# Local attention: scores of eight heads at once in contractions of 64 rows, and GpSimd's sum of the queries held back

## The reference, cut to what matters

```python
h = shift_token(x)
q, k, v = split(h @ wqkv)                      # 8 heads of 64
q = l2norm(q) * qs; k = l2norm(k) * ksc
q, k = rotary_xpos(q, k)
sim = einsum('bhwid,bhwjd->bhwij', 8 * q, k)   # a window of 64 queries, its own and the previous 64 keys
attn = softmax(where(mask, -max, sim))
x = x + (attn @ v) @ wo
```

## Time and profile before

| | us |
|---|---|
| median of 3 runs | 2175.99 |
| lowest and highest | 2174.62, 2183.37 |
| the profiled execution | 2176.2 |
| its span (first to last instruction) | 2174.4 |
| TensorE, VectorE, ScalarE, GpSimd busy in the span | 1781.2, 1635.1, 1271.2, 957.9 |
| local transformer, about | 1297 to 2174 of the span |

### The profile page before, as it was taken

The page is one execution under the profiler, slowest core; times in us unless marked ns, Lnnn a source line. Parts: engine busy times, 40 slices in busy tenths (PEclk is TensorE's granted clock), DMA queues, the critical chain, the costliest instruction groups (busy, mean ns, idle before and its releaser), DMA issues. The chain is left out here.

```text
span 2174.4 us, 36880 instructions
## 1 busy us (share of the span) xinstructions
PE 1781.2 (82%) x12448; PEld 976.1 (45%) x12448; DVE 1635.1 (75%) x3467; ACT 1271.2 (58%) x2737; POOL 957.9 (44%) x773
## 2 busy tenths in 40 slices
PE   5888898865889998859943757999998899999875
PEld 2333333332344444424423424655655556566543
DVE  5999999995577777622235767999986689999775
ACT  5777877740344444414434236888884388888721
POOL 5777887761012222223431245555550255555311
PEclk8999999996899999959976878999999999999997
DMA  5333333312111111114235140000001000000010
GB/s 150 110 111 119 122 108 116 93 49 81 39 37 36 41 36 44 31 41 133 65 105 165 52 137 15 16 21 16 11 16 23 13 16 21 16 16 11 15 42 23
DMA packets 107401, 125.47 MB, mean 58 GB/s; under 512 B 28804, under 2 KB 79151, under 8 KB 106224
## 3 DMA queue, kind: packets, MB, share of 16 engines
q1 hardware_dynamic: 103120, 115.07, 18.7%
q0 software_dynamic: 4096, 8.06, 1.1%
HBM read 71.60 MB, written 38.11 MB: 50 GB/s over the span
## 5 line engine op out<-in xcount | busy, mean ns | idle before, releaser
L394 POOL TENSOR_TENSOR m_bu<-m_dtu,m_brow 128x1024 f32<-128x1024 f32 x128 | 299.8, 2358 | 55.6 <-DVE m_hs L818 53.9
L818 DVE TENSOR_TENSOR_SCAN m_hs<-m_ps_da,m_bu 128x1024 f32<-128x1024 f32 x128 | 292.3, 2283 | 3.0 <-POOL m_bu L394 2.5
L1363 ACT ACTIVATE a_pt<-a_ps_s 128x1024 f32<-128x1024 f32 x128 | 131.1, 1024 | 226.7 <-PE a_ps_s L1141 226.7
L523 PE MATMUL m_ps_y_ps<-m_prod,m_ident 128*128 128x512 f32 x512 | 243.1, 597 | 0.0
L2913 ACT ACTIVATE l_pe<-l_ps_s,l_nbias,l_qs 128x128 f32<-128x128 f32 x512 | 227.9, 459 | 1.6
L1480 DVE TENSOR_REDUCE a_mpad<-a_ps_s 128x4 f32<-128x1024 f32 x128 | 156.9, 1226 | 92.3 <-PE a_ps_s L1133 91.1
L1133 PE MATMUL a_ps_s<-a_heads 32*128 32x256 f32 x1024 | 187.5, 446 | 43.6 <-DVE a_mpad L1480 28.5
L670 ACT ACTIVATE m_ps_da<-m_dt,m_a_neg 128x510 f32<-128x510 f32 x256 | 166.0, 681 | 74.3 <-DVE m_hs L818 73.4
L1141 PE MATMUL a_ps_s<-a_qm,a_heads 32*128 32x256 f32 x1024 | 184.7, 437 | 1.8 <-ACT a_pt L1363 1.4
L1067 POOL TENSOR_TENSOR a_rstd<-a_ve,a_mhalf 128x2 f32<-128x2 f32 x48 | 33.8, 705 | 303.0 <-DVE a_ve L1438 163.3
L828 DVE TENSOR_TENSOR m_prod<-m_hs,m_ps_c_ps 128x1024 f32<-128x1024 f32 x128 | 153.6, 1200 | 12.1 <-PE m_ps_c_ps L509 12.1
(11 more groups left out here) (339 smaller groups left out, 4252.1 us busy)
## 6 DMA issues: line engine op xcount, KB each, us to landing
m_brow<-state_rows SPq DMA_DIRECT2D x64, 512.0 KB, 4.3
slots<-m_void SPq DMA_DIRECT2D x16, 516.0 KB, 5.4
l_near<-l_v SPq DMA_DIRECT2D x64, 128.0 KB, 2.3
e_xs<-slots SPq DMA_DIRECT2D x16, 258.0 KB, 2.8
ys<-m_void SPq DMA_DIRECT2D x8, 512.0 KB, 5.3
qk<-a_qk SPq DMA_DIRECT2D x16, 256.0 KB, 2.0
a_heads<-qk SPq DMA_DIRECT2D x64, 64.0 KB
ew_w<-in_w SPq DMA_DIRECT2D x2, 2048.0 KB, 11.8
```

The source lines that it names most:

```text
L394: nc.gpsimd.tensor_tensor(bu[s % 4][:, :, :], dtu[p][:, :, :], b2, ALU.mult).then_inc(bu_rd, 1)
L523: last = pe.matmul(y_ps[:, h, :], ident[:, :], prod[d % 3][:, h, :], start=False, stop=(s == NS - 1))
L818: dve.tensor_tensor_scan(hs[s % 4][:, :, :].rearrange("p h t -> p (h t)"), da[s % 2][:, :, :, :].rearrange("p h q t -> p (h q t)"), bu[s % ...
L1363: nc.scalar.activation(pt[t % 2][:, :, :], s2[:, :, :], ACT.Exp).then_inc(exp_rd, 1)
```

## The change

- `scores` makes all 8 heads of a chunk. `kT` loses its second plane and its zeros. Each head is its own contraction over its 64 rows: even heads (rows 0 to 63) go to the first bank of `s_ps`, odd heads (64 to 127) to the second, first and second alternating. The first chunk has 8 such products of 128 by 128, the second 16 of 64 result rows by 128 columns. Two masks are written first.
- `k_copy` is one copy of 128 partitions. The clears of `kT` are gone.
- `maxima` is one reduce of 8 heads from two banks and one product. `exps` still runs in units of four, but needs the maxima of all eight, and the next `scores` needs the exponentials of all eight.
- GpSimd's `rotary_sum` of block b waits also until VectorE has done the first division of the same chunk of block b - 1.
- The `attend` lists of TensorE, ScalarE and VectorE are in a new order, and so is the end of a layer: ScalarE copies the output of the first chunk of the last block before `p_copy` of its unit U - 2, and VectorE has both last divisions ahead of `norm_apply`.

The diff; unchanged lines, small count changes and ScalarE's and VectorE's old `attend` lists are left out:

```diff
@@ -2442,10 +2442,10 @@
-kT = [m.sb(f"kT{i}", [P, 2, NP, T]) for i in range(2)]
+kT = [m.sb(f"kT{i}", [P, NP, T]) for i in range(2)]
-top, nbias = m.sb("top", [P, HU]), m.sb("nbias", [P, 2, HU])
+top, nbias = m.sb("top", [P, NH]), m.sb("nbias", [P, NH])
@@ -2467,10 +2467,10 @@
-s_ps = [m.ps(f"s{i}") for i in range(2)]
+s_ps = m.ps("s", (P, 2, 512))
-h_ps = s_ps + t_ps
+h_ps = [s_ps[:, 0, :], s_ps[:, 1, :]] + t_ps
@@ -2542,13 +2542,13 @@
         last.then_inc(cleared, 1)
         for i in range(2):
             nc.gpsimd.memset(hT[i][:, 0:1], 0.0).then_inc(cleared, 1)
-        for i in range(2):
-            nc.gpsimd.memset(kT[i][:, :, :, :], 0.0).then_inc(cleared, 1)
         def rotary_sum(l, b, c):
             i = NCH * b + c
             pool.wait_ge(l.rot_rd[Q], i + 1)
+            if b > 0:
+                pool.wait_ge(l.pn_rd, U * (b - 1) + NU * c + 1)
             nc.gpsimd.tensor_tensor(c1[Q][:, :, :], c1[Q][:, :, :], c2[Q][:, :, :], ALU.add).then_inc(l.sum_rd[Q], 1)
         def query_norms(l, b, c):
@@ -2642,26 +2642,28 @@
                                     c1[K][:, 2 * j:2 * j + 2, :].rearrange("p h d -> p (h d)"), ident[:, :])
             last.then_inc(l.xT_mm[K], 1)
-        def scores(n, b, u):
-            l, p, c, d = at[n], b % 2, u // NU, u % NU
-            i = U * b + u
-            if d == 0:
-                pe.wait_ge(l.xT_sb[Q], NCH * b + c + 1)
-                pe.wait_ge(l.xT_sb[K], 2 * (NCH * b + c + 1))
-            at_least(pe, l.ex_rd, HU * (i - 1))
-            bank = s_ps[u % 2][:, :].rearrange("p (h k) -> p h k", h=HU)
-            pe.matmul(bank, identb[:, :], mask[:, c, :, :], start=True, stop=False, skip_group_check=True)
-            for k in range(2):
-                j = 2 * d + k
+        def scores(n, b, c):
+            l, p, i = at[n], b % 2, NCH * b + c
+            pe.wait_ge(l.xT_sb[Q], i + 1)
+            pe.wait_ge(l.xT_sb[K], i + 1)
+            at_least(pe, l.ex_rd, NH * i)
+            bank = [s_ps[:, r, :].rearrange("p (j t) -> p j t", j=NP) for r in range(2)]
+            side = [slice(r * HD, (r + 1) * HD) for r in range(2)]
+            for r in range(2):
+                pe.matmul(bank[r], identb[:, :], mask[:, c, :, :], start=True, stop=False, skip_group_check=True)
+            for j in range(NP):
                 if c == 0:
-                    last = pe.matmul(bank[:, 2 * k:2 * k + 2, :], qT[p][:, j, 0:P], kT[p][:, :, j, 0:P],
-                                     start=False, stop=True, skip_group_check=True)
+                    for r in range(2):
+                        last = pe.matmul(bank[r][:, j, :], qT[p][side[r], j, 0:P], kT[p][side[r], j, 0:P],
+                                         start=False, stop=True, skip_group_check=True)
                 else:
-                    for r in range(2):
-                        q0 = P + r * HD
-                        last = pe.matmul(bank[r * HD:(r + 1) * HD, 2 * k:2 * k + 2, :], qT[p][:, j, q0:q0 + HD],
-                                         kT[p][:, :, j, q0 - HD:q0 + HD], start=False, stop=True, skip_group_check=True)
+                    for q in range(2):
+                        q0 = P + q * HD
+                        for r in range(2):
+                            last = pe.matmul(bank[r][side[q], j, :], qT[p][side[r], j, q0:q0 + HD],
+                                             kT[p][side[r], j, q0 - HD:q0 + HD], start=False, stop=True,
+                                             skip_group_check=True)
             last.then_inc(l.s_mm, 1)
         def transpose_p(n, b, u):
@@ -2716,7 +2718,8 @@
             l = at[n]
             scores(n, b, 0)
             if not first:
-                transpose_p(n, b - 1, U - 2)
+                weigh(n, b - 1, 1)
+                transpose_p(n, b - 1, 2)
             if last < 2:
                 project(n, b + 1, 0, Q)
                 if first:
@@ -2725,25 +2728,23 @@
                     pe.wait_ge(l.res_rd, NCH * (b - 1))
                 project_v(n, b + 1, 0)
             if not first:
-                weigh(n, b - 1, U - 2)
+                weigh(n, b - 1, 2)
             turn_k(n, b, 1)
-            scores(n, b, 1)
             if last < 2:
                 project(n, b + 1, 0, K)
             if not first:
-                transpose_p(n, b - 1, U - 1)
-            if last < 2:
-                turn_q(n, b + 1, 0)
-            if not first:
+                transpose_p(n, b - 1, 3)
                 if last < 2:
                     pe.wait_ge(l.v_sb, NCH * (b + 1) + 1)
                 else:
                     pe.wait_ge(l.res_rd, NCH * (b - 1))
                 output(n, b - 1, 0)
-                weigh(n, b - 1, U - 1)
-            scores(n, b, 2)
+            if last < 2:
+                turn_q(n, b + 1, 0)
+            scores(n, b, 1)
+            if not first:
+                weigh(n, b - 1, 3)
             transpose_p(n, b, 0)
             if last < 2:
                 project(n, b + 1, 1, Q)
@@ -2756,15 +2757,10 @@
             if last < 1:
                 pe.wait_ge(l.v_sb, NCH * (b + 2))
                 transpose_r(n, b + 2)
             if last < 2:
                 turn_k(n, b + 1, 0)
-            scores(n, b, 3)
-            if last < 2:
                 project(n, b + 1, 1, K)
             transpose_p(n, b, 1)
-            if last < 2:
-                turn_q(n, b + 1, 1)
             if not first:
                 if last == 0:
                     pe.wait_ge(l.hT_sb, 2 * (b + 3))
@@ -2773,7 +2769,8 @@
                 else:
                     pe.wait_ge(l.res_rd, NCH * (b - 1) + 1)
                 output(n, b - 1, 1)
-            weigh(n, b, 1)
+            if last < 2:
+                turn_q(n, b + 1, 1)
         def transposes(n, g):
             f = ff[n]
@@ -2843,10 +2840,11 @@
                 attend(n, b)
             attend(n, NB - 2, last=1)
             attend(n, NB - 1, last=2)
+            weigh(n, NB - 1, 1)
+            transpose_p(n, NB - 1, U - 2)
+            transpose_p(n, NB - 1, U - 1)
             pe.wait_ge(at[n].res_rd, NCH * (NB - 1))
             output(n, NB - 1, 0)
-            transpose_p(n, NB - 1, U - 2)
-            transpose_p(n, NB - 1, U - 1)
             weigh(n, NB - 1, U - 2)
             transposes(n, 0)
             weigh(n, NB - 1, U - 1)
@@ -2897,21 +2895,20 @@
-                at_least(act, l.s_mm, U * (b - 1))
-            for h in range(2):
-                rows_ = slice(h * HD, (h + 1) * HD)
-                nc.scalar.copy(kT[b % 2][rows_, h, :, c * P:(c + 1) * P],
-                               qk_ps[rows_, K, :].rearrange("p (j t) -> p j t", j=NP)).then_inc(l.xT_sb[K], 1)
+                at_least(act, l.s_mm, NCH * (b - 1))
+            nc.scalar.copy(kT[b % 2][:, :, c * P:(c + 1) * P],
+                           qk_ps[:, K, :].rearrange("p (j t) -> p j t", j=NP)).then_inc(l.xT_sb[K], 1)
-            act.wait_ge(l.nb_rd, i + 1)
+            act.wait_ge(l.nb_rd, NCH * b + c + 1)
-                nc.scalar.activation(pe_[u % 2][:, h, :], s_ps[u % 2][:, h * P:(h + 1) * P], ACT.Exp,
-                                     bias=nbias[:, u % 2, h:h + 1], scale=qs[b % 2][:, c, head:head + 1],
+                j = head // 2
+                nc.scalar.activation(pe_[u % 2][:, h, :], s_ps[:, head % 2, j * P:(j + 1) * P], ACT.Exp,
+                                     bias=nbias[:, head:head + 1], scale=qs[b % 2][:, c, head:head + 1],
@@ -2928,39 +2925,32 @@
             nc.scalar.copy(oT[c][:, :, :], o_ps[:, :].rearrange("p (j t) -> p j t", j=NP)).then_inc(l.oT_sb, 1)
         def attend(n, b, first=False, last=0):
-            if not first:
...
+            for c in range(NCH):
+                if not first:
+                    o_copy(n, b - 1, c)
+                if c == 1:
+                    p_copy(n, b, 0)
+                elif not first:
+                    p_copy(n, b - 1, 2)
+                exps(n, b, 2 * c)
+                if last < 2:
+                    v_copy(n, b + 1, c)
+                if c == 1 and last < 1:
+                    shift(n, b + 2)
+                if last < 2:
+                    square(n, b + 1, c, Q)
+                if c == 0:
+                    k_copy(n, b, 1)
+                elif last < 2:
+                    k_copy(n, b + 1, 0)
+                exps(n, b, 2 * c + 1)
+                if c == 1:
+                    p_copy(n, b, 1)
+                elif not first:
+                    p_copy(n, b - 1, 3)
+                if last < 2:
+                    q_copy(n, b + 1, c)
+                    square(n, b + 1, c, K)
         def affine(n, g):
             f = ff[n]
@@ -3060,18 +3050,17 @@
-        def maxima(n, b, u):
-            l, c, d = at[n], u // NU, u % NU
-            i = U * b + u
+        def maxima(n, b, c):
+            l, i = at[n], NCH * b + c
-            if d == 0:
-                dve.wait_ge(l.qs_rd, NCH * b + c + 1)
+            dve.wait_ge(l.qs_rd, i + 1)
```

(80 more changed lines are left out.)

23 lines of the change are left out of this document (3 added, 20 removed).

## The result

The changed kernel takes **2207.49 us** (median of 4 runs, 2206.7 to 2208.24); the kernel before, run beside it, 2175.73. The ratio is 1.0138, with a 95% interval from 1.0115 to 1.0162: slower, by 32 us, beyond the 0.5% that can be told from no change. The profiled execution took 2206.7 us, span 2204.9, against 2176.2 and 2174.4.

A forecast was written before the change was run, and what follows sets the result against it. No engine is full: a loop of waits sets the period, with VectorE nearly the bound. 2176.2 us, + 9.8 for the new order with the layers' ends, + 5 for clock falls, gives 2191; range 2170 to 2222.

The forecast's parts named there:

- 1 and 2, scores and maxima: In each chunk: halved score products save 0.85 us; one reduce of 1024 takes 1.226, exponentials start at 1.46.
- Rival (b): Scores: the row halves do not overlap, about +1.4 us a block, total 2222; chance 0.10.
- 3, the keys' copy: ScalarE: one copy over 128 partitions takes 0.59 us for 1.18, so 0.59 off the keys' loop.
- 4, the hold: GpSimd's sum waits for VectorE's first division: costs nothing, takes 0.86 us off the division.
- 5, the order: New engine orders: first chunk 9.73 us, second 11.10 with the shift ahead of the keys' copy; block +0.52.
- rival (a): Second chunk: the shift hides in idle ScalarE time, chunk 9.73 us, total 2150; chance 0.13.
- Blocks 1 to 13: These blocks in two layers: 26 times 0.52 us longer, +13.5.
- block 14: This block has no shift, so it gets shorter: -1.7 us over two layers.
- The first blocks: First block: scores of eight heads at half clock, longer second chunk and slower array, +4 us.
- 5, the last block: Last block, maxima to feed-forward's first affine: 16.8 us, or 18.3 at half clock, for 20.6; about -3 each, -6.
- 6, the clock: TensorE's empty stretch in second chunks: four falls of the clock at 1.3 us each, +5.
- Rival (c): TensorE's clock falls in every block, +34 us, total 2220; chance 0.13.

The follow-up runs named there:

- e6: e5 with each head's scores again contracted over all 128 rows against zero-padded keys; 2290.3 us, ratio 1.0506.
- e5: e3 with the copy of the keys again made in two halves of 64 partitions; 2211.34 us, ratio 1.0138.
- e1: The changed kernel without GpSimd's wait for the first division; 2205.1 us, ratio 1.0128.
- e7: The kernel before with only GpSimd's wait for the division added; 2179.36 us, ratio 0.9993.
- e8: e3 without GpSimd's wait for the division; 2153.84 us, ratio 0.9873.
- e2: The changed kernel with ScalarE's shift moved behind the copy of the keys; 2169.36 us, ratio 0.9958.
- e3: e2 with TensorE also turning the keys before it waits for the values' copy and transposes for the shift; 2154.18 us, ratio 0.9892.
- e4: The changed kernel with TensorE weighing the block's first unit three times over in each second chunk; 2190.98 us, ratio 1.006.

## Why the prediction was right, and which terms were off

The forecast was slower, 2191 us; it came to 2207, inside the range but 16 us above the number.

**1 and 2, scores and maxima: right.** Eight heads' products take 1.10 to 1.16 us where 1.05 was taken (0.85 and 0.2 of filling), and e6 shows the overlap itself (1.95 without). Rival (b) falls, and its price of 1.4 a block was what e6's undisturbed chunks measured; its total of 36 us was not, since in e6 the clock falls with it. The rule of the Trainium skill on weight loads (TensorE: Matmul & The Clock Gate, LDWEIGHTS) would have made it an estimated 1.7 us for the 16 loads of a first chunk one after the other; loads and products together end within 1.16, so for two row halves this trace disagrees with that reading of it. That the rows don't change the length of a single load, as it says, agrees (0.19 us for 64 and for 128 rows). From the start of the second mask to the first product it is 1496.19 - 1495.88 = 0.31 in the first chunk, as taken. The reduce of 1024 took 1.21 us.

**3, the keys' copy: right.** 0.58 for one; e5 prices the second half at 0.62 a chunk on the loop.

**4, the hold: right.** All divisions last 0.69, GpSimd's sum 1.27, and e1, e7 and e8 find no gain and no cost. That the long division ended about when the sum did was read loosely: by the earlier trace rows it ended 0.54 us later, as in e1.

**5, the order: right in kind and in size.** First chunk 9.83 (9.73 forecast), second 11.00 (11.10), block 20.83 (20.83); that the block is met to the hundredth is luck, two misses of 0.10 that cancel. The keys' copy begins 5.60 after the maxima, the point at which the forecast and rival (a) parted. VectorE's idle time ahead of the keys' rotary is 1.14 and 1.28 + 0.97 (1.0 and 2.4 forecast). e2 and e3 undo the mechanism: they are what rival (a) describes, 2150 by its sum and 2154 on the chip. Blocks 1 to 13 gave 13.8 us beside their falls (13.5), block 14 -1.4 (-1.7). The first blocks gave 2.2 us beside their falls, where 4 were taken; in e4, where the clock holds in their second chunks, they gave 1.0, so their two falls cost over 2 us each.

**5, the last block: wrong.** The step "about -3 each, -6" brought nothing: 0 around the first layer's end and +0.5 at the second's. The kernel after, timeline of the end of layer 1:

```profile
1658.19 1.72 PE L2676 MATMUL l_ps_t<-t_ident,l_pn 128*128 128x128 f32 x8
...
1659.70 1.91 PE L2713 MATMUL l_ps_a<-t_wo,l_oT 128*128 128x128 f32 x8
...
1663.00 0.78 ACT L2959 ACTIVATE l_fT<-l_ps_qk,t_lb,t_lg 128x512 f32<-128x512 f32 x1 [2.48 <-PE l_ps_qk L2780]
```

From the maxima (1643.95) to the affine it is 19.05 us, 1.5 less than the 20.57 up to the row, not 3 less, since transposes and output run at the half clock. The 1.5 were then lost again up to the start of layer 2. The windows of the kernel after over this stretch, and of e4 over the same (columns as above), with e4's affine:

```profile
1643.95:1663.00 19.05, 13.64 (x161) 11.26 (x158) 10.09 (x30) 12.79 (x42) 2.92 (x3) 0.91 0.04 11
```
```profile
1637.33:1656.33 19.00, 14.35 (x194) 11.51 (x189) 10.16 (x30) 14.21 (x45) 2.91 (x3) 1.00 0.05 11
```
```profile
1654.78 0.78 ACT L2959 ACTIVATE l_fT<-l_ps_qk,t_lb,t_lg 128x512 f32<-128x512 f32 x1 [1.46 <-PE l_ps_qk L2780]
```

In e4 the affine comes 17.45 us after the maxima (1637.33), 3.1 less than before, at a granted 1.00; e3 has 17.47, also at 1.00. So the 3 us were there, and the clock took half of them in each layer, a loss that the steps of the forecast had at 1.5 (18.3 for 16.8) and its -3 counted only in part. In e4 the two ends as a whole, counted from the maxima of block 15, are 2.4 and 1.2 us shorter than before, so some 4 of the 6 us were lost to the clock; what is lost behind the affine is open. No run changed the ends alone.

**6, the clock: right in kind, mis-sized.** The term was four falls at 1.3, +5. There were eight, at 1.66: 13.3. The number four had nothing behind it but the likeness to one stretch in the earlier trace rows. The price was near: the range of 0.9 to 1.7 held the 1.54 in the chunk, the projection alone lost 0.69 (0.86 taken), and 0.12 in the chunk behind was left out. Rival (c), a fall in every block, did not come, but e6 shows such a kernel.

These make up the 16 us: falls +8.3, ends +6.5, start of the local part +2.1, first blocks -1.8, block 14 +0.3. The start stays open: the first maxima came at 1325.82 in place of 1323.71, and in e1, which differs only by the hold, at 1323.9. It lies between 1323.7 and 1326.6 in all these kernels, with no part of the change in it that I can name; single executions of the kernel before alone differ by 9 us in all (2174.62 to 2183.37), so it need not be the change.

## What to carry to other kernels

On an engine with a queue in program order, a step that waits for another engine must stand behind whatever closes the loop: one misplaced step of 1.3 us (0.53 of waiting and two short copies) turned a 1% gain into a 1.4% loss, with every engine's busy time down. Before paying to free a blocked engine, look at what it waits for next: 0.86 us of blocked VectorE per chunk was worth nothing in three kernels. Where TensorE's work is thinned out, price the clock with it.

## What the runs showed of the hardware that I had not expected

More work for TensorE made the kernel faster: e4 has 512 records more than the kernel after and takes 16.5 us less, since the granted clock stays at the 2.4 GHz level. Yet the falls do not follow the amount of work alone: e6 has longer products than e5 and its clock falls in nearly every block, in layer 1 at first in the first chunks (12.93), later in the second ones (12.65), in layer 2 the other way round. In the kernel after they came in blocks 0, 1, 5 and 10 of both layers, alike to 0.03 us. What picks these blocks is open; so is why in e5 it is the first chunks that fall.
